# Expert stage of a graph layer: GpSimd stores a pair's result before it fetches the next input, with three result buffers in place of two

## The reference, cut to what matters

```python
x_flat = x.reshape(-1, D_MODEL)                      # layer-normed, 6250 x 256
gate_logits = x_flat @ Wg + bg + bias                # 8 experts
topk_vals, topk_idx = jax.lax.top_k(gate_logits, TOP_K)          # 2 of 8
topk_w = jax.nn.softmax(topk_vals, axis=-1)
combine = (jax.nn.one_hot(topk_idx, NUM_EXPERTS, dtype=x.dtype) * topk_w[..., None]).sum(axis=1)
h = jax.nn.relu(jnp.einsum('td,edh->teh', x_flat, W1) + b1)      # 256 -> 512
y = jnp.einsum('teh,ehd->ted', h, W2) + b2                       # 512 -> 256
out = jnp.einsum('ted,te->td', y, combine)
```

## Time and profile before

| | |
|---|---|
| median of three runs | 2764.19 us |
| the profiled execution: its own time | 2768.48 us |
| its span in the trace | 2766.5 us |
| granted TensorE clock, mean over the span | 0.942 |
| GpSimd's first gather starts | 2338.34 us |
| first give starts | 2363.36 us |
| last gather starts | 2700.81 us |
| last give starts | 2740.39 us |

### The profile page before, as it was taken

The page is one execution under the profiler, slowest core; times in us unless marked ns, Lnnn a source line. Parts: engine busy times, 40 slices in busy tenths (PEclk is TensorE's granted clock), DMA queues, the critical chain, the costliest instruction groups (busy, mean ns, idle before and its releaser), DMA issues. The chain is left out here.

```text
span 2766.5 us, 54041 instructions
## 1 busy us (share of the span) xinstructions
PE 2358.7 (85%) x19629; PEld 2076.7 (75%) x19630; DVE 2155.0 (78%) x2608; ACT 1408.7 (51%) x1924; POOL 449.8 (16%) x308
## 2 busy tenths in 40 slices
PE   0898346999999999999999999999999682999994
PEld 0555235888888888888888888888888682999984
DVE  4675488889888888898888889998867647766663
ACT  0342377555555556555555565555433122766662
POOL 0542200000000000000000000000000032788883
PEclk9998768999999999999999999999999855999997
DMA  4220300000000000000000000000000271444455
GB/s 120 50 58 22 120 0 0 1 0 0 15 0 0 3 13 0 0 14 1 0 0 15 0 0 1 14 0 0 1 1 0 88 220 33 73 77 75 76 76 127
DMA packets 106505, 89.60 MB, mean 32 GB/s; under 512 B 43340, under 2 KB 100407, under 8 KB 106164
## 3 DMA queue, kind: packets, MB, share of 16 engines
q1 hardware_dynamic: 84916, 58.87, 7.6%
q0 software_dynamic: 21504, 29.49, 6.8%
HBM read 47.91 MB, written 46.82 MB: 34 GB/s over the span
## 5 line engine op out<-in xcount | busy, mean ns | idle before, releaser
L769 PE MATMUL bank<-window,block_sb 128*128 128x256 f32 x4802 | 1115.2, 384 | 6.0 <-issue 6.0
L769 PEld LDWEIGHTS bank<-window,block_sb 128*128 128x128 f32 x4802 | 887.7, 191 | 113.9 <-issue 6.8
L974 DVE TENSOR_TENSOR hot_w<-hots,cur 128x2688 bf16<-128x2688 bf16 x343 | 534.4, 1558 | 11.9
L843 ACT COPY block_sb<-bank 128x512 f32<-128x512 f32 x343 | 201.2, 586 | 643.8 <-PE bank L761 643.7
L761 PE MATMUL bank<-hot_w,hots 128*128 128x128 bf16 x7203 | 458.8, 219 | 59.8 <-DVE hot_w L974 56.3
L761 PEld LDWEIGHTS bank<-hot_w,hots 128*128 128x128 bf16 x7203 | 420.9, 98 | 117.2 <-DVE hot_w L974 85.4
L811 ACT COPY field_rep<-fields 128x3332 bf16 (+1 forms) x151 | 383.4, 2544 | 0.0
L970 DVE TENSOR_TENSOR hots<-iota_j,cur 128x1792 bf16<-128x1792 bf16 x343 | 371.7, 1084 | 7.8 <-issue 5.5
L1248 POOL MEMSET ones<- 128x128 bf16 x1 | 0.2, 205 | 1879.4 <-POOLq L1041 1879.4
L991 DVE TENSOR_TENSOR acc<-acc,bank 128x256 f32 (+1 forms) x343 | 142.7, 416 | 200.4 <-PE bank L769 200.4
L952 DVE TENSOR_TENSOR vals<-hot_t,field_rep 128x3332 bf16<-128x3332 bf16 x100 | 236.1, 2367 | 7.7 <-PE bank L748 7.7
(11 more groups left out here) (228 smaller groups left out, 3041.1 us busy)
## 6 DMA issues: line engine op xcount, KB each, us to landing
xn_dram<-xn SPq DMA_DIRECT2D x49, 128.0 KB, 1.7
window<-xn_dram SPq DMA_DIRECT2D x7, 896.0 KB, 5.0
base_dram<-acc SPq DMA_DIRECT2D x1, 6272.0 KB, 22.3
sum_dram<-acc SPq DMA_DIRECT2D x1, 6272.0 KB, 20.3
z_dram<-acc SPq DMA_DIRECT2D x1, 6272.0 KB, 27.5
out_dram<-sum_dram SPq DMA_DIRECT2D x1, 6250.0 KB, 22.0
acc<-in_x_dram SPq DMA_DIRECT2D x1, 6144.0 KB
w_all<-in_L_ffn_W_dram SPq DMA_DIRECT2D x8, 512.0 KB, 9.9
```

What stands on the lines that cost most here:

```text
L769: mm = pe.matmul(sum_ps[pp], block_sb[pp][:, j, :], window[par][:, j, :], start=(j == 0), stop=(j == GRP - 1))
L843: act.copy(block_sb[pp][:, 0:4, :].rearrange("p m c -> p (m c)"), banks[2 * pp][:, :])
L974: dve.tensor_tensor(hot_w[i % 4][:, :, :, :].rearrange("p f g (b r) -> p f g b r", r=REP), hot[:, SRC, :, :].rearrange("p g (b r) -> p g b ...
```

## The change

GpSimd now issues `give(j)` before `gather(j+6)`. `gather` no longer waits for `z_turned`: the wait for `share_done` of the same pair covers it, since the shares are computed after `low_z`, which follows the transposes. `give(j)` waits once for both tiles of the pair, before its first DMA, in place of once for each. `y` has three buffers in place of two; `take_y(j)` so waits for the landing of pair j-3. The other buffers move up in the array `acc` by the room of one result; no size of an instruction changes.

```diff
-        y = [acc[:, X + 2 * i:X + 2 * i + 2, :] for i in range(2)]
+        y = [acc[:, X + 2 * i:X + 2 * i + 2, :] for i in range(3)]
...
             def gather(j):
                 if j >= ZB:
-                    pool.wait_ge(z_turned, j - ZB + 3)
                     pool.wait_ge(share_done, j - ZB + 1)
...
                 if j > 0:
                     pool.wait_ge(y_out, 32 * j)
+                pool.wait_ge(y_done, 2 * j + 2)
                 for n in range(2):
-                    pool.wait_ge(y_done, 2 * j + n + 1)
                     pool.indirect_dma_start(out=sum_dram, out_offset=bass.IndirectOffsetOnAxis(ap=target[:, 2 * j + n:2 * j + n + 1], axis=0),
-                                            in_=y[j % 2][:, n, :], in_offset=None, compute_op=ALU.add).then_inc(y_out, 16)
+                                            in_=y[j % 3][:, n, :], in_offset=None, compute_op=ALU.add).then_inc(y_out, 16)
...
             for j in range(NQ):
+                give(j)
                 if j + ZB < NQ:
                     gather(j + ZB)
-                give(j)
...
-            def take_y(j, i, e):
+            def take_y(j, i, b, e):
...
-                if not (isinstance(j, int) and j < 2):
-                    dve.wait_ge(y_out, 32 * (j - 1))
-                dve.tensor_tensor(y[i], y_ps[i][:, :].rearrange("p (n d) -> p n d", n=2),
+                if not (isinstance(j, int) and j < 3):
+                    dve.wait_ge(y_out, 32 * (j - 2))
+                dve.tensor_tensor(y[b], y_ps[i][:, :].rearrange("p (n d) -> p n d", n=2),
```

More of the change, by code:

```diff
@@ L1471, in experts @@
         b2_all = acc[:, 0:X, :]
-        y = [acc[:, X + 2 * i:X + 2 * i + 2, :] for i in range(2)]
+        y = [acc[:, X + 2 * i:X + 2 * i + 2, :] for i in range(3)]
         b1T = sb("b1T", [P, X * FC])
-        flat = acc[:, X + 4 + 2 * FC:, :].rearrange("p t d -> p (t d)")
+        flat = acc[:, X + 6 + 2 * FC:, :].rearrange("p t d -> p (t d)")
         zin = [flat[:, i * 2 * (D + 2):(i + 1) * 2 * (D + 2)].rearrange("p (n d) -> p n d", n=2) for i in range(ZB)]
@@ L1481, in experts @@
         zl = [sb(f"zl{i}", [P, 2, P2], F32R) for i in range(2)]
-        h = [acc[:, X + 4 + FC * i:X + 4 + FC * (i + 1), :] for i in range(2)]
+        h = [acc[:, X + 6 + FC * i:X + 6 + FC * (i + 1), :] for i in range(2)]
         hh = [sb(f"hh{i}", [P, FC, P2], F32R) for i in range(2)]
@@ L1682, in take_y @@
                 for n in range(2):
-                    dve.tensor_scalar(y[i][:, n, :], y[i][:, n, :], share[:, bass.ds(2 * j + n, 1)], None, ALU.mult).then_inc(y_done, 1)
+                    dve.tensor_scalar(y[b][:, n, :], y[b][:, n, :], share[:, bass.ds(2 * j + n, 1)], None, ALU.mult).then_inc(y_done, 1)
             def run(q, n):
@@ L1694, in run @@
                         low_h(j + 1, (i + 1) % 2)
-                    take_y(j, i % 2, e[i])
+                    take_y(j, i % 2, i % 3, e[i])
             dve.wait_ge(bias_in, 32)
```

## The result

The changed kernel takes 2776.89 us (median of 7 runs, 2769.59 to 2780.23) against 2767.12 us before (7 runs, 2762.54 to 2768.59): a ratio of 1.0035, with a 95% interval of 1.0021 to 1.0048. The forecast was 2756 us; what came is its rival on the slower side.

A forecast was written before the change was run, and what follows sets the result against it. GpSimd was taken to bound the last stage, 6.91 us a pair. Start and end +0.7, waits 0, place of `w1l` and `hl` -12, sweep +3.5 summed to -7.8 us: 2756.4 against 2764.19 us, range 2746 to 2773.

The forecast's parts named there:

- rival on the slower side: Last stage: second `hl` holds the first give, 2770 to 2785 us, chance 0.13; all slower outcomes together 0.17.
- GpSimd bounds the stage, waits cost nothing, a third buffer alone gives nothing: Last stage: GpSimd full at 6.91 us a pair; fewer waits 0 us; a third buffer by itself gives GpSimd nothing.
- The undisturbed pair of 6.40 us and the holds by `w1l` and `hl`: GpSimd's middle 40 pairs: 256.0 us undisturbed, 276.4 in the trace; holds by these instructions stretch each pair 0.5 us.
- Needs something 0.13 us after its start: GpSimd DMAs: each needs something 0.13 us after starting; if `w1l` or `hl` holds it, the DMA waits to their end.
- E': End of the second give in GpSimd's next round, E + 6.5; first give's free moment put at E' + 3.0 to 3.2.
- Start and end, +0.7 us: Last stage's ends: first give waits for the second multiply, +0.3 us; last gather between gives 49 and 50, +0.4 us.
- The way there, +3.5 us: Some five more pairs while VectorE gains lead, `w1l` and `hl` sweeping over GpSimd's round: +3.5 us.
- VectorE goes behind the gather, not the buffer: After the change the gather's landing, perhaps 2.0 us after its end, sets VectorE's place; the result buffer doesn't bind.
- The place: `w1l` and `hl` in GpSimd's round: `w1l` at E' + 0.65, holds 0.2 in place of 0.5 us a pair, -12 us.
- E: End of the second give of pair j on GpSimd, from which the prediction counted its times.
- The multiply doesn't hold it: VectorE's result multiply inside a GpSimd give: doesn't hold it, shown by the give at 2508.37 taking 1.62 us.
- second `hl` holds the first give: Rival: second `hl` starting before E' + 3.05 holds the first give up to 0.69 us; 2770 to 2785 us, chance 0.13.

The follow-up runs named there:

- e1: Kernel before with only GpSimd's order changed, give(j) ahead of gather(j+6): 2766.87 us, ratio 1.0006 to before.
- e2: Kernel before with only a third result buffer `y`: 2766.89 us, ratio 0.9998 to before.
- e3: Kernel before with only the waits changed (no `z_turned` wait, one wait per give): 2767.22 us, ratio 1.0003 to before.
- e4: Kernel before with both remainders, `w1l` and `hl`, computed on 8 columns only: 2744.17 us, ratio 0.9918 to before.
- e5: Changed kernel with both remainders, `w1l` and `hl`, computed on 8 columns only: 2745.44 us, ratio 0.9925 to before.
- e7: Changed kernel with only `hl` cut to 8 columns, `w1l` whole: 2765.21 us, ratio 0.9990 to before.
- e16: Changed kernel with VectorE and ScalarE using expert 0 throughout, not reading experts' numbers: 2764.02 us, ratio 0.9983 to before.
- e11: Kernel before with a `memset` of 128 columns ahead of each `w1l`, to start it 0.2 us later: 2766.43 us, ratio 1.0008.
- e17: Kernel before with VectorE and ScalarE using expert 0 throughout, not reading experts' numbers: 2778.11 us, ratio 1.0042 to before.
- e9: Changed kernel with `w1l` and `hl` computed in pieces of 256 columns: 2750.99 us, ratio 0.9948 to before.

## Why the prediction was wrong

- **GpSimd bounds the stage, waits cost nothing, a third buffer alone gives nothing**: right (e1 to e3).
- **The undisturbed pair of 6.40 us and the holds by `w1l` and `hl`**: right. e4 and e5 run at 1.60 and 1.00 us.
- **"Needs something 0.13 us after its start"**: it gives the lengths of the holds, but not which DMAs are held. The prediction's own row speaks against it: by it the `w1l` of 2496.20 should have held the give of 2496.22. What decides is which of the two starts first (last section), so the limit for the second `hl` was near E' + 2.85 and not 3.05.
- **Start and end, +0.7 us**: from give 49 to the last give 38.65 us against 38.29, +0.4 as said; what the give's single wait costs can't be seen beside the sweep.
- **The way there, +3.5 us**: from the first give to give 9 62.0 us against 62.4. Mis-sized, but small.
- **VectorE goes behind the gather, not the buffer**: right. The landing of the gather was 1.87 us behind its end (2442.21 to the transpose at 2444.08), inside the 1.5 to 2.5 and near the 2.0 used.
- **The place, "I take 0.2 in place of 0.5 for 41 pairs: -12 us"**: this is the step that failed. Measured in its place was 0.65 us a pair (25.9 in 40), +5.5 us. The place itself was right, 0.66 for 0.65. What failed was to take it for a resting place. I had the add of pair j+4 near E + 10.9, 6.3 us behind the transpose, and the next `zl` near E + 12.4, and did not see that the add, the two multiplies and `zl` then just touch. The add came 6.78 us behind it (2444.08 to 2450.86), waiting for TensorE, and the multiplies, counted at 0.62 us, took 0.85 under GpSimd's give. And I had the second `hl` at 0.2 to 0.4 us behind the first give's moment as if that were room, where one second gather held 0.4 us longer uses it up. From there one hold makes the next, in three rounds, and most starts of six steps begin it anew, where I had counted only 0.5 us once. The second gather, counted at 0.15 us a pair, took 0.27 (11.0 in 40), and the first give, counted as free, 0.17 (6.8 in 40).
- **"The multiply doesn't hold it"**: wrong as said. The give read for it had begun before the multiply. The give of 1.69 above shows that one which starts before the give does. Worse for the forecast is the other direction, which it left out: a give holds multiplies that fall into its middle.
- **The rival "second `hl` holds the first give"** named the mechanism, the place (before E' + 3.05) and 2770 to 2785 us, and got 0.13. It needed no early gather, as I had it, only a late second gather. Nor is it the larger part: with `hl` out of the way (e7) 15.6 of the 25.9 us of stretch stay.

What stays open: why the round doesn't settle even without the starts (e16); why e11's shift gained nothing in the kernel before, when e17's shift the other way cost 10 us; whether the changed waits add anything; and the size of the loss, which was 9.8 us in one set of runs and 5.1 in the other.

## What to carry to other kernels

Where one engine is full and is held for moments by another, the time hangs on where their instructions meet, and a change that removes 80 us of waits elsewhere can still cost. Don't compute such a place once and take it as given: ask what moves when one of the holds happens, and whether the next round comes back to the same place. Rather than aim for a free place, make the holding instructions short: the same work in pieces of 256 columns took the changed kernel 0.5% and the one before 0.3% under the time before, where moving things around gave between -0.2 and +0.4%.

## What the runs showed of the hardware that I had not expected

A GpSimd indirect DMA was held by a `w1l` or `hl` only when that one had started first. In the two traces, before and after, each of the 35 that started 0.05 to 0.29 us ahead of a DMA and ran into it held it, and none of the 18 did that started between 0.04 us ahead and 0.12 us behind, though all of them ran 0.13 us after its start (counted where the profile shows the instruction by itself). Two pairs from the trace after, GpSimd's DMA and the `w1l` beside it:

```profile
2657.16 2.06 POOL L1521 DMA_INDIRECT acc<-z_dram,token  x1 [0.30 <-DVE share L1660]
2469.02 0.98 POOL L1521 DMA_INDIRECT acc<-z_dram,token  x1 [0.31 <-issue]
```
```profile
2657.11 1.23 DVE L1664 TENSOR_TENSOR w1l<-w_all,w1h 128x1024 fp32r<-128x1024 f32 x1
2468.99 1.28 DVE L1664 TENSOR_TENSOR w1l<-w_all,w1h 128x1024 fp32r<-128x1024 f32 x1 [0.16 <-issue]
```

A held DMA then lasts to the end of the `w1l` and for its usual length less 0.13 us (2.28 for 1.58 us in e17, 0.82 + 1.46). This held for the multiply as well, which reads one tile and the share from SBUF (1.69), and apparently for a `memset` followed by `hl` (2.42). GpSimd got in between two of VectorE's instructions that follow without a pause if they are `w1l` or `hl` (e9: no more than 5.5 us in 160 DMAs; e17: the held give was let go at the end of `w1l`, with `hl` right behind it), but not between that `memset` and `hl`.

The other way round, a `w1l` that started 0.4 us into a DMA was neither delayed (1.23 us, as elsewhere) nor held it. The two multiplies were delayed: where they started 0.25 to 0.63 us into a give (in 7 of the 40 pairs before and 12 after) they took 0.71 to 0.95 us, while the ones that started up to 0.24 us into one took 0.62.

The Trainium skill, page "SBUF — State Buffer", section "Who interferes with whom", says of VectorE's two-port modes that whoever issues first gets the shared ports for the whole instruction and that the other blocks. The traces agree, for the two-input instructions too, in that a VectorE instruction that was first holds the DMA to its own end. They don't for a DMA that was first: it kept no `w1l` out, and the multiplies only for up to 0.33 us.
